# First stage of a fused two-layer kernel: the first layer's weight transposes in the place of three filler matmuls

## The reference

```python
# layer 0, "cond": a weight scaled by the condition, rows normalised
w = scale * weight[:, :, :, 0] * y[:, None, :]
dnorm = rsqrt(sum(w * w, axis=2, keepdims=True) + 1e-08)
w = w * dnorm
x_mixed = einsum('boi,bil->bol', w, E)          # E is x reshaped
# layer 0, "ffn": three linear maps in a row, then tanh
h = x_mixed @ weight @ aux_weight1 @ aux_weight2
x = x + tanh(h + bias)
# layer 1: attention over x (softmax of Q2 K2), then a fake-quantised gated FFN
x = x + ffn(attention(cond, x))
```

## Time and profile before

| | us |
|---|---|
| median of three runs | 227.13 |
| lowest, highest run | 226.79, 228.68 |
| the profiled execution, its own time | 226.91 |
| span of the profiled execution | 225.1 |
| PE busy in it | 214.6 (95%) |
| DVE busy | 163.6 (73%) |
| ACT busy | 121.0 (54%) |
| POOL busy | 108.0 (48%) |

### The profile page before, as it was taken

The page is one execution under the profiler, slowest core; times in us unless marked ns, Lnnn a source line. Parts: engine busy times, 40 slices in busy tenths (PEclk is TensorE's granted clock), DMA queues, the critical chain, the costliest instruction groups (busy, mean ns, idle before and its releaser), DMA issues.

```text
span 225.1 us, 3971 instructions
## 1 busy us (share of the span) xinstructions
PE 214.6 (95%) x1524; PEld 183.0 (81%) x1524; DVE 163.6 (73%) x340; ACT 121.0 (54%) x203; POOL 108.0 (48%) x124
## 2 busy tenths in 40 slices
PE   7999789999999999999999999999999899997993
PEld 3899779889999999999999999999999544462381
DVE  1655852885678659778697776958678789998984
ACT  3578615355134927336182461814518879897880
POOL 8426702143000535309569295683962044882684
PEclk9999979999999999999999999999999999999999
DMA  6991000480000000000000000000000000000027
GB/s 181 320 342 48 0 0 4 136 270 4 3 0 0 3 0 3 0 1 3 1 0 3 0 0 3 0 0 3 0 0 3 1 0 4 0 0 0 3 102 271
DMA packets 7402, 9.63 MB, mean 43 GB/s; under 512 B 836, under 2 KB 5464, under 8 KB 7384
## 3 DMA queue, kind: packets, MB, share of 16 engines
q1 hardware_dynamic: 6768, 8.85, 11.5%
q10 hardware_dynamic: 296, 0.53, 0.8%
q0 software_dynamic: 320, 0.01, 0.1%
HBM read 7.29 MB, written 2.10 MB: 42 GB/s over the span
## 4 chain that ended last, share of the span: by engine, by line
PE 83%; DVE 11%; ACT 2%; issue 1%; POOL 0%; DVEq 0%; ACTq 0%
PE ps L1179 53%; PE ps L1538 9%; PE ps L1163 3%; PE ps L1375 2%; PE ps L1212 2%; PE ps L1230 2%; PE ps L1623 2%; PE ps L1427 2%; DVE hmax L966 2%; DVE spread L723 1%; PE ps L1608 1%; DVE downT L812 1%; PE ps L1340 1%; PE ps L1663 1%; PE ps L1346 1%
## 5 line engine op out<-in xcount | busy, mean ns | idle before, releaser
L524 ACT ACTIVATE prob<-prob 128x512 f32<-128x512 f32 x32 | 19.8, 620 | 35.5 <-DVE prob L835 35.5
L1113 POOL TENSOR_TENSOR ptl<-prob,pth 128x512 fp32r<-128x512 f32 x16 | 20.3, 1297 | 36.6 <-ACT pth L436 36.6
L1179 PE MATMUL ps<-xh,x1h 128*128 128x256 f32 x128 | 37.2, 290 | 0.0
L1179 PE MATMUL ps<-xh,x1l 128*128 128x256 f32 x128 | 36.1, 282 | 0.0
L1179 PE MATMUL ps<-xl,x1h 128*128 128x256 f32 x128 | 36.1, 282 | 0.0
L1179 PE MATMUL ps<-vh,ptl 128*128 128x258 f32 x112 | 31.7, 283 | 0.0
L812 DVE TENSOR_REDUCE downT<-ps 128x256 f32<-128x1024 f32 x16 | 19.5, 1217 | 12.2 <-PE ps L1179 12.2
L1113 POOL TENSOR_TENSOR ptl<-prob,xh 128x512 fp32r<-128x512 f32 x13 | 16.5, 1298 | 17.8 <-ACT xh L436 17.8
L1179 PEld LDWEIGHTS ps<-xh,x1h 128*128 128x128 f32 x128 | 24.4, 191 | 0.2
L1179 PEld LDWEIGHTS ps<-xl,x1h 128*128 128x128 f32 x128 | 24.4, 191 | 0.1
L1179 PEld LDWEIGHTS ps<-xh,x1l 128*128 128x128 f32 x128 | 24.4, 191 | 0.0
(11 more groups left out here) (265 smaller groups left out, 616.8 us busy)
## 6 DMA issues: line engine op xcount, KB each, us to landing
result<-yst SPq DMA_DIRECT2D x7, 256.0 KB, 2.2
xn<-in_x SPq DMA_DIRECT2D x2, 512.0 KB, 8.5
wdn<-in_L_ffn_w_down SPq DMA_DIRECT2D x1, 704.0 KB, 7.5
wgn<-in_L_ffn_w_gate SPq DMA_DIRECT2D x1, 640.0 KB, 4.4
wun<-in_L_ffn_w_up SPq DMA_DIRECT2D x1, 640.0 KB, 5.2
xn<-in_x ACTq DMA_DIRECT2D x2, 256.0 KB, 5.0
a<-in_L_ffn_aux_weight SPq DMA_DIRECT2D x2, 256.0 KB, 6.1
xn<-in_x SPq DMA_DIRECT2D x2, 256.0 KB, 6.6
```

What stands on the lines that cost most here:

```text
L524: act.activation(prob[:, 2 * k:2 * k + 2, :], prob[:, 2 * k:2 * k + 2, :], ACT.Exp, scale=ATT_SCALE).then_inc(p_ready, 1)
L1113: pool.tensor_tensor(ptl[:, g % 2, 2 * k:2 * k + 2, :], prob[:, 2 * k:2 * k + 2, :], pth[g % 2][:, 2 * k:2 * k + 2, :].bitcast(F32), ALU.s ...
L1179: last = pe.matmul(dst, a, b, start=(n == 0), stop=(n == len(passes) - 1))
```

## The change

PE's three filler matmuls (`warm(WARM1)`) are dropped. The four transposes of `wf` move up from behind the row sums into their place, with their waits on `ycol_ready` and `ld_wf`. ACT's copy of the result (`wfT`) moves ahead of the root of the row sums. The other lists stay as they are.

```diff
@@ the constants
-    WARM0, WARM1 = 6, 3
+    WARM0 = 6
@@ ScalarE: row_norms()
                 act.wait_ge(wl_ps, 1)
                 act.activation(flat(wsq[:]), ps[:, 6, :], ACT.Square).then_inc(wsq_ready, 1)
+                act.wait_ge(wfT_ps, 1)
+                copy(wfT, blocks(3), wfT_ready)
                 act.wait_ge(s2_ready, 1)
                 act.activation(col("rt", 0, 4), col("s2", 0, 4), ACT.Sqrt).then_inc(rt_ready, 1)
...
             row_norms()
-            act.wait_ge(wfT_ps, 1)
-            copy(wfT, blocks(3), wfT_ready)
             x0_hi(0)
@@ TensorE
             pe.wait_ge(ld_mix, 16)
             square_T(6, wl).then_inc(wl_ps, 1)
-            warm(WARM1)
+            pe.wait_ge(ycol_ready, 1)
+            pe.wait_ge(ld_wf, 16)
+            square_T(3, wf).then_inc(wfT_ps, 1)
             pe.wait_ge(wsq_ready, 1)
             pe.wait_ge(y2_ready, 1)
...
             last.then_inc(ss_ps, 1)
             pe.wait_ge(ycol_ready, 1)
-            pe.wait_ge(ld_wf, 16)
-            square_T(3, wf).then_inc(wfT_ps, 1)
             x_T(0)
```

## The result

The changed kernel takes 228.81 us (median of 20 runs, 226.48 to 229.29); the kernel before takes 227.57 us over 20 runs of the same comparison (225.20 to 229.58). The ratio is 1.0072 with a 95% interval of 1.0044 to 1.0100: slower by 0.7%. Ratios leave out executions that lie over 1.5% above the fastest one of their kernel; since here a single kernel spreads that wide by itself, the counts further down take all executions. The two medians, over all executions, differ by 0.5%.

The account below looks back on a forecast made before the run. PE was taken to bound the kernel (83% of the chain); its first-stage terms gave -0.54 us, of which x's landing left -0.07: 226.84 from 226.91, 227.06 from the median, so 226.9 us, range 225.8 to 228.8.

Parts of the forecast that it names:

- the one on the wf transposes: Moved wf transposes on PE start at 5.66 us, about two at each clock level, taking 0.75 us instead of 0.50.
- The time of the rise: PE's clock goes from 1.2 to 2.4 GHz near 6.2 us, placed by the longest row-sum weight load, 337 ns.
- First rival: PE's clock rises later, slowing wf transposes, row sums and x's transposes: +1.65 us, 228.5; chance 0.21.
- the worse form: PE's clock rises only with the wide products behind x's transposes, slowing these too: +1.78 us more, 230.2; chance 0.06.
- The wait for x: x's second piece lands at 7.62 us and holds x's transposes, leaving 0.07 us of about half a microsecond gained.
- The rule on transposes: Transposes don't engage PE's full clock, so moved ones can't replace the fillers that raise it near 6.2 us: 228.5.
- Third rival, wf late: wf's transfer lands at 7.11 us instead of 5.61, delaying PE's moved transposes: +1.0 us, 228.0; chance 0.06.
- Fourth rival, the later dip: The low-clock stretch after PE's idle time to 29.20 us, costing 1.7 us, goes away: 225.1; chance 0.06.
- ACT and the row scales: ACT's wfT copy runs about 6.5 to 7.1 us without holding the root; diag stays hidden by 0.9 us: no cost.

Follow-up runs that it names:

- e6: Kernel before with two filler matmuls behind the wl transposes in place of three: median 228.46 us, ratio 1.0042 to before.
- e11: Kernel before with ten filler matmuls in PE's wait at 26.9 to 29.2 us: median 225.73 us, ratio 0.9956 to before.
- e8: The changed kernel run again with no edit, 12 runs: median 228.32 us, ratio 1.0064 to before.
- e7: Kernel before with PE waiting for wsq ahead of the three fillers and not behind them: median 230.16 us over 6 runs, no ratio given.
- e2: Changed kernel with the three fillers put back ahead of the moved wf transposes: median 226.28 us, ratio 0.9988 to before.
- e12: Kernel before with the changed order, one filler ahead of wf's transposes, three behind the row sums, ten in the wait at 26.9 us: 226.58 us, ratio 0.9956.
- e1: Kernel before with the three fillers dropped and nothing moved: median 229.14 us over 6 runs, ratio 1.0123 to before.
- e3: Kernel before with six transposes of the identity in place of the three fillers: median 227.27 us, ratio 1.0009 to before.
- e4: Changed kernel with the wf transposes done as ordinary matmuls with the identity: median 229.09 us over 6 runs, no ratio given.
- e9: Changed kernel with three fillers behind the row sums, the gap ahead of wf left open: median 229.15 us, ratio 0.9991 to before.

## Why the prediction was wrong

**The forecast (226.9).** No change was forecast, with a hair to the fast side, and 0.7% slower came. The step that failed is the one on the wf transposes, "At the new place they start at 5.66, before the clock's rise near 6.2", and "The rise near 6.2 lets about two run at each level". It took the time of the rise from the trace of before as given, when the change takes away what made PE's row unbroken up to it. The gap of 0.34 us measured was even shorter than the 0.49 in the sum. In the profiled execution the sum came out as -1.28 for the fillers, 0.35 for the wait, 0.59 for the transposes of wf, 0.53 for the row sums, 0.89 for x's transposes and 1.22 for the product: +2.30 us in place of -0.07. The last three terms stood at nothing in the forecast.

The time of the rise was also misread. The longest row-sum load (337 ns) is not the first but one that starts at 6.24, and the next still took 317; the rise lay near 6.7, and other executions have it near 4.3 (e6, e11). With 6.7 all four wf transposes would have run at the low level, 1.04 us and not 0.75. The forecast would have been the same, because x's landing at 7.62 hides the difference.

**First rival (228.5, chance 0.21).** This is what happened in 7 of the 20 executions, the profiled one among them, and in 8 of the 12 of e8. In 11 of the 20 and 4 of the 12 the corrected time says that the clock rose in time and fell once more; e8's profile shows that as a fall behind the wait for x, which no rival names. That its 228.5 lies near the median of 228.81 is therefore in part luck: two different losses have about the same price. Its chance was too low all the same. The argument against it, "the new gap is 0.49 us and not 2.3", measured a gap before the first rise by one in the middle of the program. e7 shows that 0.69 us there is enough to undo three fillers. The sizes were off in both directions: the row sums took 1.50 us and not 1.94, because part of the 0.97 that was doubled had run at the low level already, but the low level lasted through most of the product with wfT as well (3.00 us against 1.78), which the text had as the worse form (230.2). The profiled execution lies between the two, at 229.23.

**The wait for x.** The mechanism was right: x's second piece holds the transposes of x and eats what is gained ahead of them. Its size was off. The landing at 7.62 us was taken as fixed, but it lay anywhere from 7.41 (1.73 + 5.67, e11) over 7.94, 8.11 and 8.60 (e2, e8 and e12) to 8.94 (1.72 + 7.22, e1) in other profiles. What was missed is its consequence, and this is the second step that failed: the half microsecond gained does not just vanish into a wait, the wait can cost the clock (e8: 1.34 us of it, then 3.4 us at half, 1.7 us lost). The sentence "the rest becomes a wait for the transfer" put no price on that wait.

**The rule on transposes.** The rule of the Trainium skill that the prediction weighed (page "TensorE: Matmul & The Clock Gate", section "Part 4: PE-mode transpose") pointed to 228.5, close to the result, but for a reason that these runs do not bear out: in e3 transposes stand in for the fillers without a loss (1.0009), and in e4 ordinary matmuls do not rescue the changed kernel (3 late rises and 2 second stretches in 6). The row in the trace that spoke against the rule was read rightly.

**Third rival, wf late.** It did not happen: wf landed 4.2 us after its issue, 0.2 earlier than before.

**Fourth rival, the later dip.** The price was about right: 1.7 us worked out, a median 1.5 us lower in e11. The change did not remove it: the profiled execution has a mean clock of 0.992, as before.

**ACT and the row scales.** Right: the copy of wfT ran from 6.64 to 7.24 us, ahead of s2 at 8.14, and diag was ready at 9.86, long before its use near 12.9.

## What to carry to other kernels

A filler matmul that covers a wait early in a kernel is not free time to be reclaimed, and neither is work that finishes earlier only to stand in front of a transfer. Before moving work into such a place, ask whether PE stays busy without a break both up to the clock's rise and until the next transfer lands; if not, keep a filler in each gap (here one of 0.43 us and three short ones took the changed kernel from 30 bad executions in 32 to 1 in 12). And read more than one execution: the clock's course varied between executions of the same program by 3 us or more.

## What the runs showed of the hardware that was not expected

- A gap of 0.34 us on PE at 5.2 us was followed by 6.8 us of busy PE at half clock before the rise (the changed kernel's profile); with a gap of 0.69 us and three wide matmuls behind it, by over 7 (e7). In other executions a gap of 0.18 us (e8) or 0.29 (e9) there did not put the rise off. A wait of 1.34 us at the full clock was followed by 3.4 us at half (e8).
- The first rise came between about 4.3 us (e6, e11) and 6.7 us (before) with the same instructions ahead of it up to 4.1 us.
- PE's row of two-column matmuls counts as busy in the profile, yet it stood in each of the stretches in which the clock failed to rise. Whether it is part of the cause was not tried.
- The recorded granted clock leaves out the low level ahead of the first rise, so that an execution can read 0.998 and still take 228.20 us (changed kernel), where one of before with 0.999 took 225.33. Durations of one repeated shape (421 and 272 ns) show it.
